# Sharing one low-rank partial product between the two token halves of a tile

## The chip, the cores and the metric

The kernel runs on one core of one Trainium2 chip. The metric is the device time of one execution in microseconds (us), as the median of several runs. A profile of one execution stands beside it: the span from the first to the last instruction of the core, what each engine did in it, and who waited for whom.

## The reference

The input is u, 2 x 1024 tokens of width 512. The network is

```
x = u
x = x + 0.5 * ffn(layernorm(x))
x = x + s4(layernorm(x))          # convolution of length 512 along the width, plus D * input
x = x + 0.5 * ffn(layernorm(x))   # the same weights again

def qlinear(x, q, scale, A, B):   # q: integers 0..15
    return x @ ((q - 7.5) * scale * 0.005).T + 0.02 * (x @ A @ B)
def ffn(x):                       # 512 -> 1376 -> 512, low rank R = 32
    h = silu(qlinear(x, gate)) * qlinear(x, up)
    return qlinear(h, down)
```

What matters here is x @ A for the gate and the up projection together. The two matrices A have 32 columns each. The kernel calls this product P.

## The kernel before, in words

The 2048 tokens are four tiles of 512. Each tile goes through the feed-forward part twice, so there are N2 = 8 tile passes, n = 0 to 7; the convolution is worked in between, in the passes 2 to 5. This text calls a pass simply a tile. A tile has four sub-tiles of 128 tokens, i = 0 to 3.

Every number that TensorE multiplies is split into a high and a low part in fp16. For A both parts lie side by side in `a_w`, 128 columns in all (gate high, up high, gate low, up low; 4 * R), one block of rows for each 128 of the width.

Tiles 0 and 1 are multiplied plainly (`plain_blocks`). From tile 2 on (`FAST = 2`) gate and up are computed by a scheme with seven products of half-size blocks (`fast_blocks`). Its operands lie transposed in `xT`: B11 and B21 are the upper and lower half of the width for the first 256 tokens, B22 is the lower half for the second 256 tokens, and T1 is the upper half for the second 256 tokens minus B11. So the second tokens' upper half isn't there itself; it is T1 + B11.

A tile n is two stages. In the first, 11 blocks m of 128 inner features are multiplied (L1402, `part`), with the low-rank terms added by `low_rank` (L1365) from `PT`, the transposed P of the tile. In the second, the down stage, `down_pass` (L1323) multiplies the hidden features, four sub-tiles j with a wide and a narrow half each. Between the passes of the down stage stand small pieces of work, in an order written out by hand for each engine in its function `tile`:

- `pd_high` (ACT, L616), `pd_split` (DVE, L904), `pd_transpose` (PE, L1335), `pd_copy` (ACT, L624), `down_low` (PE, L1342): the low-rank term of the down projection, for each j. `down_low` needs what `pd_copy` wrote.
- `p_product(n + 1, i)` (PE, L1288): P of the next tile, sub-tile i, into one bank of PSUM. `p_high` (ACT, L597) takes its high part into `p_stack`, `p_split` (DVE, L897) its low part, and SP's queue then transposes it by a DMA into `PT`. `p_product(i)` waits until `p_split(i - 1)` is done, since both use the same bank. In the tiles from 2 on the four sub-tiles are taken in the order 0, 2, 1, 3 of the tokens (`sub`), so i = 0 and 2 are of the first 256 tokens, i = 1 and 3 of the second.
- `down_read`, `down_add` (DVE, L943, L955, L958): the residual sum into X. `conv_product` and `conv_add`: the convolution. `conv_stats`, `ln_stats`: sums for the normalisations.

Each engine takes its instructions strictly in order. At the end of the down stage the order on ACT is p_high(3), pd_copy(3); after the second pass it is p_high(1), pd_copy(1). On PE, `down_low(3)` is the last instruction ahead of the next tile's first block.

Of the kernel before, what the change touches and what calls it, by code (L numbers as in the profile page):

```python
# [19 lines left out]
P = 128  # L20
# [12 lines left out]
def s4_macaron(nc, x_d, state_d, step_d, gq_d, uq_d, dq_d, scales_d, ds_d, a_d, b_d, da_d, db_d,  # L33
# [39 lines left out]
    with ExitStack() as ctx:  # L73
# [125 lines left out]
        tab = view(ring, 0, P, 2, KH, L)  # L199
        phase, ptmp, toep = view(ring, 4096, P, 2, KH, P), view(ring, 5120, P, 2, P), view(ring, 5376, P, L)  # L200

        cz16 = view(ring, 0, P, TS, 2, H, dt=F16)
        czs = view(ring, 2048, P, 2, H)
        czT = view(ring, 3072, P, TS, 2, KH, P, dt=F16) if False else \
# [51 lines left out]
        class Ffn:  # L256
# [3 lines left out]
            def __init__(self):  # L260
                def s(what):
                    return sem(f"ffn_{what}")

                def two(what):
                    return [s(f"{what}_{b}") for b in range(2)]

                self.agg, self.var, self.rstd = s("ln_aggregated"), s("ln_var"), s("ln_rstd")
                self.zs, self.zhi, self.z16 = s("zs"), s("z_hi"), s("z16")

                self.z_d, self.z_t = s("z_differences"), s("z_sums")  # L270
                self.zq_hi, self.zq_lo = s("z_quarters_hi"), s("z_quarters_lo")
                self.tp0, self.xT0 = s("first_x_transposed"), [s(f"first_xT{j}_ready") for j in range(4)]
                self.xT = [s(f"xT_sub{j}_ready") for j in range(4)]
                self.xTq = two("xT_quarters_ready")
                self.p_mm, self.p_hi, self.p_stack = s("p_mm"), s("p_hi"), s("p_stack")
                self.p_t0, self.PT0 = s("first_p_transposed"), s("first_PT_ready")
                self.PT = two("PT_ready")
                self.pd_mm, self.pd_hi, self.pd_stack = s("pd_mm"), s("pd_hi"), s("pd_stack")
                self.pd_t, self.pd_out = s("pd_transposed"), s("PdT_ready")

                self.g_mm, self.gl_mm, self.u_mm, self.ul_mm = s("g_mm"), s("gl_mm"), s("u_mm"), s("ul_mm")
                self.tg, self.tu = two("gate_scaled"), two("up_scaled")

                self.p1, self.p5, self.p6, self.p3, self.p7 = (s(f"product_{i}") for i in (1, 5, 6, 3, 7))
                self.t11, self.t5, self.t12, self.t21 = (s(f"sum_{i}_copied") for i in ("11", "5", "12", "21"))
                self.up_s, self.gate_s = s("up_sums_scaled"), s("gate_sums_scaled")
                self.lr_gate, self.lr_up = s("low_rank_gate_mm"), s("low_rank_up_mm")
# [291 lines left out]
        def _(act):  # L579
# [8 lines left out]

            def p_high(n, i):

                act.wait_ge(f.p_mm, n * TS + i + 1)
                if n * TS + i < TS + 2:
                    after(act, f.p_t0, n * TS + i - 1)
                else:
                    act.wait_ge(f.PT[i % 2], (n - 1) * 32 + i // 2 * 16)
                for slot, part in ((0, 0), (3, 0), (2, 1)):
                    last = nc.scalar.activation(  # L597
                        p_stack[:, i % 2, :, slot, :],
                        p_bank(n, i)[:, part * 2 * R:(part + 1) * 2 * R].rearrange("p (g r) -> p g r", g=2),
                        ACT.Copy, scale=P_SCALE / (Z_SCALE * A_SCALE))  # L600
                last.then_inc(f.p_hi, 1)

# [204 lines left out]
        def _(dve):  # L807
# [73 lines left out]
            def z_step(n, m):  # L881
# [9 lines left out]
                elif m in (4, 10):  # L891
                    z_sums(n, m // 10)

            def p_split(n, i):

                dve.wait_ge(f.p_hi, n * TS + i + 1)
                V.scalar_tensor_tensor(p_stack[:, i % 2, :, 1, :],  # L897
                                       p_bank(n, i)[:, 0:2 * R].rearrange("p (g r) -> p g r", g=2),
                                       P_SCALE / (Z_SCALE * A_SCALE), p_stack[:, i % 2, :, 0, :],
                                       ALU.mult, ALU.subtract).then_inc(f.p_stack, 1)  # L900

# [15 lines left out]
            def h_low(n, m):  # L917
                b, r = m % 2, rows[m]
                dve.wait_ge(f.hhi[b], uses(n, m) + 1)
                V.tensor_tensor(hT[0:r, m, 1, :], h32[0:r, b, :], hT[0:r, m, 0, :], ALU.subtract)\  # L920
                    .then_inc(f.hlo[b], 1)
# [99 lines left out]
            def tile(n):  # L1021

                more, s4, c = n + 1 < N2, n + 1 == FAST, conv_group(n)
                (plain_blocks if n < FAST else fast_blocks)(n)
                h_low(n, M - 1)
                pd_split(n, 0)
                down_read(n, 0)
                pd_split(n, 1)
                if more:
                    p_split(n + 1, 0)  # L1030
                down_read(n, 1)
                down_add(n, 0)
                if n == 0:
                    s4_b_copy()
                if more:
                    p_split(n + 1, 1)
                pd_split(n, 2)
# [12 lines left out]
                    s4_scale()  # L1050
                if c is not None:
                    conv_add(c * TS + 2)
                if more:
                    p_split(n + 1, 2)
                pd_split(n, 3)
# [3 lines left out]
                    s4_vectors()  # L1059
                if s4:  # L1060
                    s4_split()
                if more:
                    p_split(n + 1, 3)
                down_read(n, 3)
# [189 lines left out]
        def _(pe):  # L1254
# [14 lines left out]
            def p_product(n, i):  # L1269

                s = sub(n, i)
                if n == 0:
                    pe.wait_ge(f.xT0[i], 1)
                elif n < FAST:
                    pe.wait_ge(f.xT[i], n * 16)
                else:
                    pe.wait_ge(f.xTq[i // 2], (n - FAST + 1) * 32)
                if not (n == 0 and i < 3):
                    pe.wait_ge(f.p_stack, i - 2 if n == 0 else n * TS + i)
                if n < FAST:  # L1280
                    terms = [(xT_plain[:, a, c, s * P:(s + 1) * P], c) for c in range(KH) for a in range(2)]
                else:
                    j = s % 2
                    ops = ((B11, 0), (B21, 2)) if s < 2 else ((T1, 0), (B11, 0), (B22, 2))
                    terms = [(xT[:, a, 2 * op + k, j * P:(j + 1) * P], c + k)
                             for op, c in ops for k in range(2) for a in range(2)]
                for t, (x, c) in enumerate(terms):
                    last = mm(p_bank(n, i)[:, 0:4 * R], x, a_w[:, c, :], start=(t == 0), stop=(t == len(terms) - 1))  # L1288
                last.then_inc(f.p_mm, 1)

            def p_transpose(j):
# [355 lines left out]
```

## Time and profile before

| | |
|---|---|
| Median of 3 runs | 592.99 us (592.35 to 594.93) |
| The profiled execution's own time | 592.97 us |
| Span of the profiled execution | 591.2 us |
| Granted TensorE clock, mean | 0.994 |
| PE busy | 570.9 us, 97% |
| DVE busy | 410.8 us, 69% |
| ACT busy | 303.3 us, 51% |
| POOL busy | 238.5 us, 40% |

PE is TensorE's multiplications, PEld its weight loads, DVE VectorE, ACT ScalarE, POOL GpSimd, SP the engine that issues most DMAs. In the rows below, "L897 DVE ... p_stack<-banks,p_stack" is one instruction of line 897 that writes p_stack from PSUM (banks) and p_stack. An arrow in square brackets says how long the engine stood idle before the instruction and what ended that. Matmuls are pipelined, so the end of one is modelled and overlaps the next: the time that a matmul costs is read from the starts.

### The profile page before, as it was taken

The numbers are of one execution on the slowest core, as the hardware profiler recorded it, in microseconds if no ns is written. First come the engines' busy times: TensorE is split into PE (matmuls) and PEld (weight loads), VectorE is DVE, ScalarE is ACT, GpSimd is POOL, SyncE is SP. The second block draws the span as 40 slices with busy tenths as digits, with TensorE's granted clock in tenths as the row PEclk, the third lists the DMA queues.
The fourth block names the chain that finished last, engine by engine and source line by source line (L and its number), as shares of the span: only waits on it lengthen the run. The fifth ranks groups of instructions, "written<-read, shape, count | busy, mean of one in ns | idle before, by whom it ended". The sixth has DMA issues, their size and how long they took to land.

```text
span 591.2 us, 12188 instructions
## 1 busy us (share of the span) xinstructions
PE 570.9 (97%) x4674; PEld 439.0 (74%) x4674; DVE 410.8 (69%) x768; ACT 303.3 (51%) x748; POOL 238.5 (40%) x245
## 2 busy tenths in 40 slices
PE   7799999999989999999999999999999999999997
PEld 6444675436568887788878887788877888788975
DVE  6578876697288885698675995469844788446544
ACT  5576322655117871288514785057831586236621
POOL 5447802031204881058800597015850367105510
PEclk8999999999999999999999999999999999999999
DMA  8991302203300066000730019200190201630001
GB/s 274 373 372 23 72 10 58 95 0 67 65 14 1 1 82 125 11 1 7 129 72 10 2 19 147 42 11 1 19 183 11 77 1 32 104 136 17 1 2 72
DMA packets 86009, 40.50 MB, mean 69 GB/s; under 512 B 74592, under 2 KB 78880, under 8 KB 85952
## 3 DMA queue, kind: packets, MB, share of 16 engines
q1 hardware_dynamic: 85136, 39.59, 28.4%
q8 instruction: 37, 0.61, 0.4%
q10 hardware_dynamic: 816, 0.14, 0.1%
q14 instruction: 20, 0.16, 0.1%
HBM read 17.43 MB, written 4.19 MB: 37 GB/s over the span
## 4 chain that ended last, share of the span: by engine, by line
PE 88%; SPq 3%; DVE 3%; DMA 2%; ACT 2%; issue 1%; DVEq 1%; POOL 0%; ACTq 0%
PE banks L1402 34%; PE banks L1323 28%; PE banks L1383 9%; PE banks L1365 5%; PE banks L1536 4%; PE banks L1288 3%; DMA X<-in_x 2%; PE banks L1342 2%; SPq L333 1%; PE banks L1359 1%; PE banks L1519 1%; SPq L332 1%; ACT p_stack L597 1%; DVEq L817 1%; ACT PdT L624 0%
## 5 line engine op out<-in xcount | busy, mean ns | idle before, releaser
L1402 PE MATMUL banks<-xT,w 128*128 128x256 f16 (+1 forms) x1848 | 223.1, 273 | 1.3 <-DVE ring L955 1.3
L1402 PEld LDWEIGHTS banks<-xT,w 128*128 128x128 f16 (+1 forms) x1848 | 182.0, 100 | 22.7 <-issue 1.7
L1323 PE MATMUL banks<-dw,hT 128*128 128x256 f16 (+3 forms) x1408 | 184.4, 286 | 0.0
L1323 PEld LDWEIGHTS banks<-dw,hT 128*128 128x128 f16 (+1 forms) x1408 | 135.4, 98 | 34.5 <-issue 0.6
L914 DVE SCALAR_TENSOR_TENSOR work<-banks,work 128x512 f32<-128x512 f32 (+1 forms) x88 | 60.6, 689 | 53.4 <-PE banks L1365 24.9
L1383 PE MATMUL banks<-xT,w 128*128 128x512 f16 (+1 forms) x336 | 80.7, 385 | 2.1 <-ACT work L646 1.1
L446 POOL TENSOR_TENSOR rstd<-veps,minus_half 128x1 f32<-128x1 f32 x32 | 20.7, 648 | 151.5 <-DVE veps L820 151.3
L510 POOL TENSOR_SCALAR hT<-work 128x512 f16<-128x512 f32 x60 | 38.0, 633 | 89.0 <-DVE work L914 88.9
L513 POOL TENSOR_TENSOR hT<-work,hT 128x512 f16<-128x512 f32 x60 | 71.0, 1183 | 5.0
L1383 PEld LDWEIGHTS banks<-xT,w 128*128 128x128 f16 (+1 forms) x336 | 33.3, 101 | 43.2 <-ACT work L646 3.1
L597 ACT ACTIVATE p_stack<-banks 128x64 f16<-128x64 f32 x96 | 14.6, 225 | 88.0 <-PE banks L1288 84.6
L520 POOL TENSOR_TENSOR z<-zs,z 128x1024 f16<-128x1024 f32 (+1 forms) x24 | 46.9, 1964 | 25.5 <-ACT z L671 25.5
L928 DVE SCALAR_TENSOR_TENSOR banks<-banks,scales,work 128x512 f32<-128x512 f32 (+1 forms) x66 | 49.5, 750 | 2.2 <-PE banks L1402 2.2
L935 DVE SCALAR_TENSOR_TENSOR banks<-banks,scales,work 128x512 f32<-128x512 f32 (+1 forms) x66 | 49.5, 750 | 0.7 <-ACT work L728 0.4
L714 ACT ACTIVATE work<-banks,scales 128x256 f32<-128x256 f32 (+1 forms) x66 | 31.3, 475 | 26.6 <-PE banks L1402 26.6
L728 ACT ACTIVATE work<-banks,scales 128x256 f32<-128x256 f32 (+1 forms) x66 | 31.2, 473 | 25.2 <-PE banks L1402 25.0
L653 ACT ACTIVATE work<-banks 128x512 f32<-128x512 f32 (+1 forms) x66 | 39.4, 597 | 5.2 <-PE banks L1365 5.2
L635 ACT ACTIVATE banks<-banks,scales 128x512 f32<-128x512 f32 (+1 forms) x44 | 28.9, 657 | 22.7 <-PE banks L1383 22.5
L897 DVE SCALAR_TENSOR_TENSOR p_stack<-banks,p_stack 128x64 f16<-128x64 f32 x32 | 7.2, 224 | 47.9 <-ACT p_stack L597 47.9
L710 ACT ACTIVATE work<-banks,scales 128x256 f32<-128x256 f32 (+1 forms) x66 | 31.3, 474 | 7.1 <-PE banks L1402 7.1
L717 ACT ACTIVATE work<-banks,scales 128x256 f32<-128x256 f32 (+1 forms) x66 | 31.3, 474 | 0.0
L904 DVE SCALAR_TENSOR_TENSOR pd_stack<-banks,pd_stack 128x32 f16<-128x32 f32 x32 | 6.0, 189 | 36.2 <-ACT pd_stack L616 36.0
(167 smaller groups left out, 708.8 us busy)
## 6 DMA issues: line engine op xcount, KB each, us to landing
out_x<-X SPq DMA_DIRECT2D x16, 256.0 KB, 2.7
X<-in_x SPq DMA_DIRECT2D x1, 2048.0 KB, 14.0
ring<-in_tables SPq DMA_DIRECT2D x1, 2048.0 KB, 9.1
ring<-in_gate_q_t SPq DMA_DIRECT2D x2, 768.0 KB, 13.0
hT<-in_up_q_t SPq DMA_DIRECT2D x2, 768.0 KB, 13.0
work<-in_b SPq DMA_DIRECT2D x2, 688.0 KB, 9.5
X<-in_x SPq DMA_DIRECT2D x4, 256.0 KB, 5.5
X<-in_x SPq DMA_DIRECT2D x1, 1024.0 KB, 12.5
```

The source lines that it names most:

```text
L510: pool.tensor_scalar(hT[0:r, m, 0, :], h32[0:r, b, :], 1.0, 0.0, ALU.mult, ALU.add)\
L513: pool.tensor_tensor(hT[0:r, m, 1, :], h32[0:r, b, :], hT[0:r, m, 0, :], ALU.subtract)\
L520: pool.tensor_tensor(z16[:, j, 1, ops, :], zs[:, ops, :], z16[:, j, 0, ops, :], ALU.subtract)\
L653: nc.scalar.activation(silu[0:r, b, :].rearrange("p (c t) -> p c t", c=2), gate_sums(m), ACT.Silu, scale=LR_OUT).then_inc(f.silu[b], 1)
L710: nc.scalar.activation(t_up[s][0:r, 0, :], sums, ACT.Copy, scale=scales[0:r, 1, m:m + 1])\
L714: nc.scalar.activation(t_gate[s][0:r, 1, :], bank[4 * s + 1][0:r, 0:HH], ACT.Copy, scale=scales[0:r, 0, m:m + 1]).then_inc(f.t5, 1)
L914: V.scalar_tensor_tensor(shape(h32[0:r, b, :]), up, H_SCALE * LR_OUT, shape(silu[0:r, b, :]), ALU.mult, ALU.mult).then_inc(f.h[b], 1)
L928: V.scalar_tensor_tensor(up_sums(m), up_sums(m), scales[0:r, 1, m:m + 1], t_up[s][0:r, :, :], ALU.mult, ALU.add).then_inc(f.up_s, 1)
L935: V.scalar_tensor_tensor(gate_sums(m), gate_sums(m), scales[0:r, 0, m:m + 1], t_gate[s][0:r, :, :], ALU.mult, ALU.add).then_inc(f.gate_s, 1)
L1323: last = mm(acc(j)[:, 1 - c, 0:width], hT[0:rows[m], m, a, j * P:(j + 1) * P], dw[0:rows[m], m, src], start=(m == 0 and a == 0), stop=(m = ...
L1383: last = mm(dst[0:r, :], wg[:, c, cols], xT_plain[:, a, c, :], start=(c == 0 and a == 0), stop=(c == KH - 1 and a == 1))
L1402: last = mm(dst[0:r, 0:HH], w[:, blocks + k, cols], xT[:, a, 2 * op + k, :], start=(first and k == 0 and a == 0), stop=(k == 1 and a == 1) ...
```

## The change

For the tiles from 2 on, the upper half of A times B11 is multiplied once for each 128 first tokens and stays in PSUM, in the first 128 columns of the bank. The own part of each sub-tile goes beside it, in columns of its own: for i = 0 and 2 the lower half (B21), for i = 1 and 3 T1 and B22. The product of i = 1 uses the B11 sums that i = 0 left, that of i = 3 those that i = 2 left. An even i has 8 matmuls as before, an odd i has 8 for 12.

The sum of both parts is made by DVE in a new step, `p_sum(n + 1, i)`: it copies the own part from PSUM to `p32` in SBUF, waits for that copy, and adds the shared part from PSUM to it. `p_high` and `p_split` then read `p32`. `p_high` waits for `p_summed` where it waited for `p_mm`. `p_sum` stands on DVE directly ahead of each `p_split` of a tile from 2 on.

```diff
@@ view of SBUF @@
+        p32 = view(ring, 7168, P, 4 * R)
@@ p_high(n, i) @@
-                act.wait_ge(f.p_mm, n * TS + i + 1)
+                if n < FAST:
+                    act.wait_ge(f.p_mm, n * TS + i + 1)
+                else:
+                    act.wait_ge(f.p_sum, (n - FAST) * TS + i + 1)
+                src = p_bank(n, i) if n < FAST else p32
@@ new, on DVE @@
+            def p_sum(n, i):
+
+                k = (n - FAST) * TS + i
+                dve.wait_ge(f.p_mm, n * TS + i + 1)
+                after(dve, f.p_hi, n * TS + i)
+                own = slice(4 * R * (1 + i % 2), 4 * R * (2 + i % 2))
+                V.tensor_copy(p32, p_bank(n, i)[:, own]).then_inc(f.p_own, 1)
+                dve.wait_ge(f.p_own, k + 1)
+                V.tensor_tensor(p32, p_bank(n, i)[:, 0:4 * R], p32, ALU.add).then_inc(f.p_sum, 1)
@@ tile(n) on DVE, and likewise for 1, 2 and 3 @@
+                if fast:
+                    p_sum(n + 1, 0)
                 if more:
                     p_split(n + 1, 0)
@@ p_product(n, i) on PE @@
                 if n < FAST:
-                    terms = [(xT_plain[:, a, c, s * P:(s + 1) * P], c) for c in range(KH) for a in range(2)]
+                    last = sums(0, [(xT_plain[:, a, c, s * P:(s + 1) * P], c) for c in range(KH) for a in range(2)])
+                elif i % 2 == 0:
+                    sums(0, half(B11, 0))
+                    last = sums(1, half(B21, 2))
                 else:
-                    j = s % 2
-                    ops = ((B11, 0), (B21, 2)) if s < 2 else ((T1, 0), (B11, 0), (B22, 2))
...
+                    last = sums(2, half(T1, 0) + half(B22, 2))
                 last.then_inc(f.p_mm, 1)
```

The order of instructions on three engines shows what has moved. First PE at the end of the down stage of tile 3, before. L1288 is the product of sub-tile 3, L1335 and L1342 are `pd_transpose(3)` and `down_low(3)`, and L1402 is the first block of the next tile. What an instruction waits for stands in brackets.

```order
L1288 MATMUL banks_3<-a_w,xT 128x128 [waits ffn_p_stack,ffn_xT_quarters_ready_1]
L1288 MATMUL banks_3<-a_w,xT 128x128 x11
L1335 MATMUL banks_1<-ident,pd_stack 128x128 [waits ffn_dsum,ffn_PdT_ready,ffn_pd_stack]
L1323 MATMUL banks_5<-dw,hT 128x256 x4
L1342 MATMUL banks_1<-db_w,PdT 128x512 [waits ffn_dsum,ffn_PdT_ready]
L1402 MATMUL banks_3<-xT,w 128x256 [waits conv_out,ffn_p_stack,ffn_silu_0,ffn_xT_quarters_ready_1,ffn_xT_quarters_ready_0]
```

The rows after the change are the same but for the count: the first product of the group is followed by 7 and not 11.

```order
L1310 MATMUL banks_3<-a_w,xT 128x128 [waits ffn_p_stack,ffn_xT_quarters_ready_1]
L1310 MATMUL banks_3<-a_w,xT 128x128 x7
```

ACT at the same place, after the change: L624 is `pd_high(3)` there, L605 `p_high(3)` and L632 `pd_copy(3)`.

```order
L624 ACTIVATE pd_stack<-banks_5 128x32 [waits ffn_pd_transposed,ffn_pd_mm]
L624 ACTIVATE pd_stack<-banks_5 128x32 x2
L605 ACTIVATE p_stack<-ring 128x2x32 [waits ffn_PT_ready_1,ffn_p_summed]
L605 ACTIVATE p_stack<-ring 128x2x32 x2
L632 ACTIVATE PdT<-banks_1 128x128 [waits ffn_dl_mm,ffn_pd_transposed]
```

The order on ACT is as before; `p_high` waits for DVE's sum in place of PE's product, and `pd_copy` still stands behind it.

DVE in the second half of the down stage of tile 1, before. L897 is `p_split` of the sub-tiles 2 and 3, and L1210 to L1213 are `s4_split`, which is done once, in this tile.

```order
L897 SCALAR_TENSOR_TENSOR p_stack<-banks_1,p_stack 128x2x32 [waits ffn_p_hi]
L904 SCALAR_TENSOR_TENSOR pd_stack<-banks_5,pd_stack 128x32 [waits ffn_pd_hi]
L1210 RECIPROCAL k_scale<-k_scale 128x1 [waits s4_kernel_scale_ready]
L1211 TENSOR_SCALAR ring<-ring,k_scale 128x512 [waits dve_s4_step]
L1212 CAST ring<-ring 128x512 [waits dve_s4_step]
L1213 TENSOR_TENSOR ring<-ring 128x512 [waits dve_s4_step]
L897 SCALAR_TENSOR_TENSOR p_stack<-banks_1,p_stack 128x2x32 [waits ffn_p_hi]
L943 TENSOR_TENSOR work<-banks_5,d_scale 128x512 [waits ffn_dsum,ffn_d_mm_1]
L955 SCALAR_TENSOR_TENSOR ring<-banks_3,work 128x512 [waits ffn_d_read_1,ffn_x_updated,ffn_dl_mm]
```

And after the change, where L916 is `p_split`:

```order
L908 COPY ring<-banks_1 128x128 [waits ffn_p_hi,ffn_p_mm]
L910 TENSOR_TENSOR ring<-banks_1,ring 128x128 [waits ffn_p_own_copied]
L916 SCALAR_TENSOR_TENSOR p_stack<-ring,p_stack 128x2x32 [waits ffn_p_hi]
L923 SCALAR_TENSOR_TENSOR pd_stack<-banks_5,pd_stack 128x32 [waits ffn_pd_hi]
L1238 RECIPROCAL k_scale<-k_scale 128x1 [waits s4_kernel_scale_ready]
L1239 TENSOR_SCALAR ring<-ring,k_scale 128x512 [waits dve_s4_step]
L1240 CAST ring<-ring 128x512 [waits dve_s4_step]
L1241 TENSOR_TENSOR ring<-ring 128x512 [waits dve_s4_step]
L908 COPY ring<-banks_1 128x128 [waits ffn_p_hi,ffn_p_mm]
L910 TENSOR_TENSOR ring<-banks_1,ring 128x128 [waits ffn_p_own_copied]
L916 SCALAR_TENSOR_TENSOR p_stack<-ring,p_stack 128x2x32 [waits ffn_p_hi]
L962 TENSOR_TENSOR work<-banks_5,d_scale 128x512 [waits ffn_dsum,ffn_d_mm_1]
```

Two instructions stand ahead of each `p_split`, and ACT's `p_high(3)`, which waited for PE alone before, comes behind all of `s4_split` through them. Over the six tiles these are 48 matmuls fewer and 48 instructions on DVE more.

## Rows read from the trace of the kernel before

**Rows 1.** The page: PE's busy time, and the shares of the last chain by engine.

```profile
PE 570.9 (97%) x4674; PEld 439.0 (74%) x4674; DVE 410.8 (69%) x768; ACT 303.3 (51%) x748; POOL 238.5 (40%) x245
PE 88%; SPq 3%; DVE 3%; DMA 2%; ACT 2%; issue 1%; DVEq 1%; POOL 0%; ACTq 0%
```

**Rows 2.** Waits, whole span: who waited for whom, us in total, times, longest.

```profile
PEld banks L1342 <- ACT PdT L624: 10.1, 31, 0.5
```

**Rows 3.** Timeline, tile 3 around P's sub-tile 1: start, us, engine, line.

```profile
301.46 0.83 PE L1288 MATMUL banks<-a_w,xT 128*128 128x128 f16 x12
...
302.13 0.22 PE L1335 MATMUL banks<-ident,pd_stack 128*128 128x128 f16 x1
...
302.19 0.71 PE L1323 MATMUL banks<-dw,hT 128*128 128x320 f16 x4
302.33 0.46 ACT L597 ACTIVATE p_stack<-banks 128x64 f16<-128x64 f32 x3 [4.88 <-PE banks L1288]
302.66 0.30 ACT L624 ACTIVATE PdT<-banks 128x128 f16<-128x128 f16 x1
...
303.00 0.10 PEld L1342 LDWEIGHTS banks<-db_w,PdT 128*128 128x128 f16 x1 [0.45 <-ACT PdT L624]
303.01 0.39 PE L1342 MATMUL banks<-db_w,PdT 128*128 128x512 f16 x1
```

**Rows 4.** Timeline, tile 3 around P's sub-tile 3, end of the tile.

```profile
317.51 0.30 ACT L624 ACTIVATE PdT<-banks 128x128 f16<-128x128 f16 x1
...
317.85 0.10 PEld L1342 LDWEIGHTS banks<-db_w,PdT 128*128 128x128 f16 x1 [0.50 <-ACT PdT L624]
```

**Rows 5.** DVE's groups by line and form: count, busy us, mean ns, idle before.

```profile
L955 DVE SCALAR_TENSOR_TENSOR ring<-banks,work 128x512 f32<-128x512 f32 x32 | 22.0, 689 | 2.2
...
L897 DVE SCALAR_TENSOR_TENSOR p_stack<-banks,p_stack 128x64 f16<-128x64 f32 x32 | 7.2, 224 | 47.9 <-ACT p_stack L597 47.9
...
L1150 DVE COPY cs<-banks 128x32 f32<-128x32 f32 x1 | 0.2, 181 | 0.0
```

**Rows 6.** ACT's groups by line and form, a source in PSUM and in SBUF.

```profile
L653 ACT ACTIVATE work<-banks 128x512 f32<-128x512 f32 x60 | 35.8, 597 | 0.7 <-PE banks L1365 0.7
L640 ACT ACTIVATE hT<-work 128x512 f16<-128x512 f32 x20 | 12.6, 631 | 12.1 <-DVE work L914 12.1
```

**Rows 7.** Timeline, tile 6, which has no convolution: P's sub-tiles 1 to 3.

```profile
514.65 0.22 DVE L897 SCALAR_TENSOR_TENSOR p_stack<-banks,p_stack 128x64 f16<-128x64 f32 x1 [1.47 <-ACT p_stack L597]
...
521.98 0.23 DVE L897 SCALAR_TENSOR_TENSOR p_stack<-banks,p_stack 128x64 f16<-128x64 f32 x1 [2.00 <-ACT p_stack L597]
...
523.15 0.77 PEld L1288 LDWEIGHTS banks<-a_w,xT 128*128 128x128 f16 x12
```

**Rows 8.** Timeline, end of tile 1 with `s4_split`.

```profile
170.87 0.23 DVE L897 SCALAR_TENSOR_TENSOR p_stack<-banks,p_stack 128x64 f16<-128x64 f32 x1 [1.12 <-ACT p_stack L597]
...
172.15 0.83 PE L1288 MATMUL banks<-a_w,xT 128*128 128x128 f16 x12
172.42 0.69 DVE L1213 TENSOR_TENSOR ring<-ring 128x512 f16<-128x512 f32 x1
173.01 0.46 ACT L597 ACTIVATE p_stack<-banks 128x64 f16<-128x64 f32 x3 [1.91 <-PE banks L1288]
...
174.46 0.69 DVE L955 SCALAR_TENSOR_TENSOR ring<-banks,work 128x512 f32<-128x512 f32 x1
...
175.40 0.82 PE L1402 MATMUL banks<-xT,w 128*128 128x256 f16 x6 [1.32 <-DVE ring L955]
```

**Rows 9.** Stretches: length, busy us of PE, PEld, DVE, ACT, POOL (count), PEclk, DMA.

```profile
98.40:101.10 2.70, 1.87 (x17) 1.82 (x16) 2.23 (x5) 1.16 (x2) 1.56 (x2) 1.00 0.12 26
101.20:102.50 1.30, 1.30 (x7) 0.56 (x7) 0.00 (x0) 0.00 (x0) 0.04 (x1) 0.93 0.83 247
102.50:105.00 2.50, 2.50 (x7) 0.88 (x6) 0.00 (x0) 1.18 (x2) 0.00 (x0) 0.50 1.02 377
105.00:106.00 1.00, 1.00 (x4) 0.39 (x3) 0.00 (x0) 0.00 (x0) 0.00 (x0) 0.64 1.04 397
```

More of the change, by code:

```diff
@@ L274, in __init__ @@
                 self.xTq = two("xT_quarters_ready")
+                self.p_own, self.p_sum = s("p_own_copied"), s("p_summed")
                 self.p_mm, self.p_hi, self.p_stack = s("p_mm"), s("p_hi"), s("p_stack")
@@ L598, in p_high @@
                         p_stack[:, i % 2, :, slot, :],
-                        p_bank(n, i)[:, part * 2 * R:(part + 1) * 2 * R].rearrange("p (g r) -> p g r", g=2),
+                        src[:, part * 2 * R:(part + 1) * 2 * R].rearrange("p (g r) -> p g r", g=2),
                         ACT.Copy, scale=P_SCALE / (Z_SCALE * A_SCALE))
@@ L892, in z_step @@
                     z_sums(n, m // 10)
+            def p_sum(n, i):
[6 more added lines that the diff above has]
+                V.tensor_tensor(p32, p_bank(n, i)[:, 0:4 * R], p32, ALU.add).then_inc(f.p_sum, 1)
             def p_split(n, i):
                 dve.wait_ge(f.p_hi, n * TS + i + 1)
+                src = p_bank(n, i) if n < FAST else p32
                 V.scalar_tensor_tensor(p_stack[:, i % 2, :, 1, :],
-                                       p_bank(n, i)[:, 0:2 * R].rearrange("p (g r) -> p g r", g=2),
+                                       src[:, 0:2 * R].rearrange("p (g r) -> p g r", g=2),
                                        P_SCALE / (Z_SCALE * A_SCALE), p_stack[:, i % 2, :, 0, :],
@@ L1025, in tile @@
                 h_low(n, M - 1)
+                fast = more and n + 1 >= FAST
                 pd_split(n, 0)
@@ L1034, in tile @@
                     s4_b_copy()
+                if fast:
+                    p_sum(n + 1, 1)
                 if more:
@@ L1052, in tile @@
                     conv_add(c * TS + 2)
+                if fast:
+                    p_sum(n + 1, 2)
                 if more:
@@ L1061, in tile @@
                     s4_split()
+                if fast:
+                    p_sum(n + 1, 3)
                 if more:
@@ L1279, in p_product, with sums, half @@
                     pe.wait_ge(f.p_stack, i - 2 if n == 0 else n * TS + i)
+                def sums(out, terms):
+                    for t, (x, c) in enumerate(terms):
+                        last = mm(p_bank(n, i)[:, out * 4 * R:(out + 1) * 4 * R], x, a_w[:, c, :], start=(t == 0),
+                                  stop=(t == len(terms) - 1))
+                    return last
+                def half(op, c):
+                    return [(xT[:, a, 2 * op + k, s % 2 * P:(s % 2 + 1) * P], c + k) for k in range(2) for a in range(2)]
                 if n < FAST:
-                    terms = [(xT_plain[:, a, c, s * P:(s + 1) * P], c) for c in range(KH) for a in range(2)]
-                else:
-                    j = s % 2
-                    ops = ((B11, 0), (B21, 2)) if s < 2 else ((T1, 0), (B11, 0), (B22, 2))
[L1285 to L1288, printed above, removed]
+                    last = sums(0, [(xT_plain[:, a, c, s * P:(s + 1) * P], c) for c in range(KH) for a in range(2)])
+                elif i % 2 == 0:
+                    sums(0, half(B11, 0))
+                    last = sums(1, half(B21, 2))
+                else:
+                    last = sums(2, half(T1, 0) + half(B22, 2))
                 last.then_inc(f.p_mm, 1)
```

## The prediction, made before the changed kernel was run

> **What bounds the kernel now.** I read the page first: PE is busy 97% of the span and makes up 88% of the chain that ended last [rows 1]. So each matmul taken away counts in full, if nothing comes in its place. Then I asked where PE does stand still, because an edit that takes 4 matmuls from a group can be lost in one short stall. The view of the waits shows it at once: the largest wait of PE's weight loads on another engine is that of `down_low` (L1342) for ACT's `pd_copy` (L624), 31 times, 0.5 us at most [rows 2]. That is a wait in the very stretches where the change works.
>
> The timeline of tile 3 shows why it is long there. P's product for sub-tile 1 issues from 301.46; PE goes on to `pd_transpose` and four matmuls of the down pass, the last steps it can take. ACT waits for the product, runs `p_high` from 302.33, and only then, in its order, `pd_copy` at 302.66, which ends at 302.96; the weights of `down_low` load at 303.00, after 0.45 us of idle weight loader [rows 3]. `pd_copy` itself had its input at 302.35, when the transpose had ended (302.13 + 0.22): it is late because it stands behind `p_high`. At sub-tile 3 the same chain ends at 317.81 and lets `down_low` go at 317.85, after 0.50 us [rows 4]; then comes the next tile. So in each fast tile two chains, product - `p_high` - `pd_copy` - `down_low`, are on the path already, with nothing to spare.
>
> **What the change removes.** 12 matmuls of 128 columns take 302.13 - 301.46 = 0.67 us from start to start, 56 ns each [rows 3]. It takes away 4 at i = 1 and 4 at i = 3, 0.22 us a site; 48 in six tiles would be 2.7 us if PE alone counted.
>
> **What it adds.** Two DVE instructions, 128 columns wide, stand between the product and `p_high`. No row has this width. A line through L897 (64 wide, 224 ns) and L955 (512 wide, 689 ns) has 1.04 ns a column, so the add is 290 ns; from the copy of 32 columns (181 ns) the same slope gives 281 ns [rows 5]. Each handover costs some 35 ns: the transpose-to-load case is `pd_copy`'s end at 302.96 to the load at 303.00, and PE's product to ACT is alike, so the one to DVE takes the place of the old one and two are new (copy to add, add to ACT). The pair is 0.28 + 0.29 + 0.07 = 0.64 us. The bounds: two copies of 32 columns would be 0.36 + 0.07 = 0.43 us, two instructions of 512 columns 1.38 + 0.07 = 1.45 us. I take 0.64, since 128 lies much nearer to 64 than to 512. `p_high` now reads SBUF: ACT's 512-wide instruction takes 631 ns from there for 597 from PSUM [rows 6], so 0.03 us more.
>
> The Trainium skill, page "VectorE: DVE Perf Modes", section "The TRN2 errata — SBUF-src ops pay a fixed extra latency per instruction", prices a VectorE instruction from PSUM at 120 cycles plus one for each element and ScalarE's at 224 from SBUF for 172 from PSUM. As an estimate by that page copy and add would be 0.52 us and not 0.57, `p_high` 0.04 us later, and my sum below 0.5 us smaller. Its figure for 64 columns would be 192 ns where the trace has 224 [rows 5], so I stay with the rows.
>
> **The sites.** At i = 1 of tile 3, `p_high` starts 0.64 - 0.22 later and `pd_copy` ends 0.45 us later (0.64 + 0.03 - 0.22); `down_low` goes with it, and with `down_low` everything behind it on PE. The same at i = 3. DVE is free when the product arrives: it stood idle before all of its 32 `p_split`s together 47.9 us [rows 5], in tile 6 at i = 1, the tightest, 1.47 us before 514.65 [rows 7], of which `p_high` and the handovers take some 0.5 and the pair of i = 0 before it pushes it 0.63, so about 0.1 is left after the 0.22 saved. The pairs at i = 0 and i = 2 are hidden: behind i = 0 nothing of PE is due for four microseconds of down pass, and behind i = 2 stands `p_product(3)`, which waits for `p_split(2)`. That ends at 522.21, with the pair at 522.88, and the product's first load is at 523.15 [rows 7]: 0.27 us are left. Behind the waiting `p_sum` on DVE stand `p_split`, `pd_split` or `down_read`, and `down_add`; DVE stood there before too, waiting for ACT, so they come later by the pair and no more, and PE's next need of each is later than that. SP's transposes of P move with `p_split`, and `PT` is first read in the next tile's second block.
>
> So each of the tiles 2 to 6 costs 2 x 0.45 = 0.90 us, and five of them 4.5 us.
>
> **Tile 1** is dearer. Its i = 1 costs 0.45 as above. At i = 2 `p_split` (170.87) comes 0.67 later again, and with it `s4_split`, which stands behind it on DVE and ended at 173.11 (172.42 + 0.69), just about when `p_high(3)` started, 173.01 [rows 8]. Before, `p_high(3)` did not depend on it. Now `p_sum(3)` comes behind it: `s4_split` ends at 173.11 + 0.44 + 0.64 = 174.19, the pair starts some 0.08 before (DVE instructions overlap by that) and `p_high(3)` starts at 174.11 + 0.64 = 174.75, 1.74 us later. The 4 matmuls saved at i = 3 gain nothing there, as PE's product (172.15) is done long before. `pd_copy`, `down_low` and `down_add` (174.46) follow, and PE's first block waits for that sum before and after (175.40, 1.32 us idle) [rows 8]. Tile 1 costs 1.77 us with ACT's 0.03.
>
> **The sum:** 13 pairs on the path (two in each of five tiles, three in tile 1) at 0.67 = 8.7 us, less 11 savings of 0.22 = 2.4 us: +6.3 us. The profiled execution took 592.97 us, 0.02 under the median of the runs, so no correction is due: 599.2 us, 1.05% slower.
>
> **The rivals.**
> - *PE alone counts.* The chains are hidden, only the 48 matmuls go: 592.97 - 2.7 = 590.3 us. For it speaks PE's 97%. Against it: the pair would have to be under 0.22 us, which is where a site turns, and two copies of even 32 columns are 0.36 us [rows 5]. Place: `down_low` at i = 1 and 3. Chance 5%.
> - *Half is given back.* The delay at i = 3 is made up in the next tile, because PE waits there for something that did not move. Then five sites go: 6.3 - 5 x 0.45 = +4.0, 597.0 us. Against it: `down_low` is the last step before the tile, and PE's stalls inside the fast blocks are tiny beside 570.9 us busy. Chance 12%.
> - *The clock falls at the end of tile 1.* PE is to stand there almost idle from about 173.6 to 177.1 but for one `down_low`. After 98.40 to 101.10, a stretch in which PE had only tiny matmuls and gaps, the granted clock was 0.93, then 0.50 (the level of 1.2 GHz), then 0.64 over the next 4.8 us [rows 9]; that lost 1.3 x 0.07 + 2.5 x 0.50 + 1.0 x 0.36 = 1.7 us. The sum becomes +8.0: 600.9 us. The Trainium skill, "TensorE: Matmul & The Clock Gate", section "Part 1: The HAM clock gate (the 'warmup' mystery)", has the throttled state as the default that activity lifts; by that rule 600.9 is the answer if the gap is long enough, and the trace shows such a fall once. Chance 15%.
> - *The pair is longer*, 0.8 us or more, by the wait for its own copy or a slower copy from PSUM: 13 x 0.16 = 2.1 more, 601.3 us, and at 0.9 `p_product(3)` of tile 6 begins to wait too. Chance 8%.
>
> **How the numbers follow.** The forecast has 60%: 599.2 us, its own range 597.9 to 600.5 with the pair 0.1 us either way (13 x 0.1). The range to hold the time 8 times in 10 goes from 596.9, which takes in half given back, to 601.2, which takes in the fall of the clock. A measurement of this kernel can tell 0.5%, 3 us, from no change: slower means above 595.96 and faster below 590.03. Forecast, clock, longer pair and two thirds of the second rival are slower: 91%. 7% are within, with most of the first rival, which lies at -0.45%. Faster 2%.
>
> **What would show it.** The wait of `down_low`'s load on `pd_copy` rises from 10.1 us by 0.67 x 11 plus 1.5 in tile 1, to about 19 us. From the first matmul of the odd P products to `down_low` there are 1.55 us in tile 3 now (301.46 to 303.01) and about 2.0 after. Copy and add show 0.28 and 0.29 us. PE's idle time before the first block of tile 2 stays at 1.3 us, with another 1.9 us before `down_low`. The fast blocks themselves, from the second block on, last as long as before. I would be wrong if `down_low` no longer waits for `pd_copy` (then less), if copy and add together take under 0.45 us, or if the granted clock behind tile 1 falls under 1.00.

## The result and the profile after

The changed kernel takes 602.19 us (median of 4 runs, 601.35 to 602.88) for 593.72 us of the kernel before on the same chip: a ratio of 1.0154, 95% interval 1.0133 to 1.0176. It is slower, as forecast, but by more: the forecast counted 6.3 us on top of 592.97, and 602.19 is 9.2 us above that number (8.5 us above the median of this comparison). 602.2 lies above the range, which ended at 601.2. The traced execution took 602.22 us, its span is 600.5 us. Of all executions below, one of e8 and one of e12 took 850 us at a mean granted clock of 0.65; the ratios leave them out.

First the waits of PE's weight loads on other engines, changed kernel, whole span: the row that answers to [rows 2]. L1377 is `down_low` and L632 `pd_copy`.

```profile
PEld banks L1377 <- ACT PdT L632: 19.9, 31, 2.2
```

It was 10.1 us with at most 0.5 in one place; 19 were forecast. The only other wait that grew by as much as a microsecond is at L1293, ahead of the fast tiles, in code that the change leaves as it was (PE's wait there is 5.4 us for 4.3). So the loss is in this one wait, and in what the wait brings about. Here is the timeline of the changed kernel in tile 3 around P's sub-tile 1, the stretch of [rows 3].

```profile
306.50 0.61 PE L1310 MATMUL banks<-a_w,xT 128*128 128x128 f16 x8
...
306.94 0.22 PE L1370 MATMUL banks<-ident,pd_stack 128*128 128x128 f16 x1
...
307.14 0.29 DVE L908 COPY ring<-banks 128x128 f32<-128x128 f32 x1 [0.48 <-PE banks L1310]
307.47 0.29 DVE L910 TENSOR_TENSOR ring<-banks,ring 128x128 f32<-128x128 f32 x1
307.80 0.55 ACT L605 ACTIVATE p_stack<-ring 128x64 f16<-128x64 f32 x3 [4.54 <-DVE ring L910]
308.25 0.26 ACT L632 ACTIVATE PdT<-banks 128x128 f16<-128x128 f16 x1
308.38 0.23 DVE L916 SCALAR_TENSOR_TENSOR p_stack<-ring,p_stack 128x64 f16<-128x64 f32 x1 [0.61 <-ACT p_stack L605]
...
308.56 0.10 PEld L1377 LDWEIGHTS banks<-db_w,PdT 128*128 128x128 f16 x1 [1.18 <-ACT PdT L632]
```

Eight matmuls in place of twelve, then copy and add at 0.29 us each, then `p_high` and `pd_copy`, and only then the load, after 1.18 us idle for 0.45 before. From the start of the copy to that of `p_high` pass 0.66 us. From the start of `p_high` to that of `pd_copy` pass 0.45 us, where they were 0.33 (302.33 to 302.66, [rows 3]), and `pd_copy` itself takes 0.26 for 0.30. So a site costs 0.66 + 0.12 - 0.04 = 0.74 us and saves 0.22.

The chain that ended last gives the start of each tile's first block: start, us, line, count. The kernel before:

```profile
175.40 5.18 PE banks L1402 x46
246.89 5.04 PE banks L1402 x46
318.25 5.04 PE banks L1402 x46
389.61 5.04 PE banks L1402 x46
460.95 5.04 PE banks L1402 x46
525.19 5.08 PE banks L1402 x46
```

And the changed kernel:

```profile
176.72 7.90 PE banks L1437 x46
251.95 5.04 PE banks L1437 x46
324.31 5.04 PE banks L1437 x46
396.69 5.04 PE banks L1437 x46
469.06 5.04 PE banks L1437 x46
534.38 5.09 PE banks L1437 x46
```

Each of these rows is one tile, from 2 to 7. A tile of the steady part takes 72.37 us (from 324.31 to 396.69, and from there to 469.06) for 71.35 before: 1.02 more, with 0.90 forecast. Tile 2 is another matter: 75.23 us for 71.49, 3.74 more, of which 2.72 are in the first 46 matmuls alone, 7.90 us for 5.18. The stretches of the changed kernel around them say why (length, busy us of PE, PEld, DVE, ACT, POOL with counts, granted TensorE clock, DMA):

```profile
173.10:176.60 3.50, 0.39 (x1) 0.10 (x1) 2.68 (x7) 0.71 (x4) 0.00 (x0) 0.84 0.13 26
176.60:182.20 5.60, 5.48 (x26) 3.94 (x27) 1.70 (x5) 1.42 (x3) 0.55 (x1) 0.50 0.02 6
182.20:184.60 2.40, 2.40 (x24) 2.14 (x22) 1.95 (x3) 1.51 (x4) 0.00 (x0) 0.98 0.00 0
```

PE had one matmul in 3.5 us, and the granted clock was 0.50, the level of 1.2 GHz, for the whole of the next 5.6 us; half of PE's 5.48 busy us there is 2.7 us. That was a rival with 15%. Only the traced execution shows where the clock fell; its mean over the span is 0.987, those of the other three are 0.990, 0.993 and 0.991. The end of tile 1 in the changed kernel, which answers to [rows 8]:

```profile
172.99 0.69 DVE L1241 TENSOR_TENSOR ring<-ring 128x512 f16<-128x512 f32 x1
173.59 0.28 DVE L908 COPY ring<-banks 128x128 f32<-128x128 f32 x1
173.91 0.29 DVE L910 TENSOR_TENSOR ring<-banks,ring 128x128 f32<-128x128 f32 x1
174.24 0.55 ACT L605 ACTIVATE p_stack<-ring 128x64 f16<-128x64 f32 x3 [2.57 <-DVE ring L910]
...
175.00 0.39 PE L1377 MATMUL banks<-db_w,PdT 128*128 128x512 f16 x1 [1.92 <-ACT PdT L632]
175.78 0.69 DVE L974 SCALAR_TENSOR_TENSOR ring<-banks,work 128x512 f32<-128x512 f32 x1
...
176.72 5.49 PE L1437 MATMUL banks<-xT,w 128*128 128x256 f16 x25 [1.33 <-DVE ring L974]
```

The copy comes directly behind `s4_split`, as forecast, and PE stands still 1.92 and 1.33 us with one matmul between.

### The profile page after: what moved, and what is told of

It is laid out like the page before. It is cut to its first block, busy times and chain, and to the rows that moved or that the text cites. A ratio compares the mean times of both kernels' runs of the same rounds, so it can differ in the third digit from the quotient of the medians.

```text
span 600.5 us, 12164 instructions
## 1 busy us (share of the span) xinstructions
PE 570.0 (95%) x4626; PEld 436.7 (73%) x4626; DVE 424.0 (71%) x816; ACT 305.1 (51%) x748; POOL 238.6 (40%) x245
## 4 chain that ended last, share of the span: by engine, by line
PE 88%; DVE 6%; ACT 2%; issue 2%; DMA 1%; DVEq 1%; POOL 0%; SPq 0%; ACTq 0%
PE banks L1437 34%; PE banks L1358 27%; PE banks L1418 10%; PE banks L1400 5%; PE banks L1571 4%; PE banks L1310 2%; PE banks L1377 2%; PE banks L1394 1%; ACT p_stack L605 1%; PE banks L1554 1%; DMA X<-in_x 1%; DVE ring L910 1%; DVE ring L908 1%; DVEq L825 1%; DVE stats L824 0%
## 5 line engine op out<-in xcount | busy, mean ns | idle before, releaser
L1437 PE MATMUL banks<-xT,w 128*128 128x256 f16 (+1 forms) x1848 | 225.8, 275 | 1.3 <-DVE ring L974 1.3
L605 ACT ACTIVATE p_stack<-ring 128x64 f16<-128x64 f32 x72 | 13.1, 245 | 80.0 <-DVE ring L910 80.0
L624 ACT ACTIVATE pd_stack<-banks 128x32 f16<-128x32 f32 x96 | 11.8, 196 | 37.1 <-PE banks L1358 37.1
```

Of the source, the lines that this page charges most:

```text
L1437: last = mm(dst[0:r, 0:HH], w[:, blocks + k, cols], xT[:, a, 2 * op + k, :], start=(first and k == 0 and a == 0), stop=(k == 1 and a == 1) ...
```

## The experiments

The theory: the pair of DVE instructions lies on the chain product, `p_high`, `pd_copy`, `down_low` at i = 1 and 3, and PE waits for its end; behind tile 1 the stretch gets so empty that the clock falls. The rivals: DVE's load as such, and a slow first block from some other source. All ratios are to the kernel before on the same chip. The times of the tiles and of the clock are from one traced execution of each kernel.

**e1: the pair without the saving.**

```diff
-                own = slice(4 * R * (1 + i % 2), 4 * R * (2 + i % 2))
+                own = slice(0, 4 * R)
...
-                V.tensor_tensor(p32, p_bank(n, i)[:, 0:4 * R], p32, ALU.add).then_inc(f.p_sum, 1)
+                V.tensor_tensor(p32, p_bank(n, i)[:, 0:4 * R], p32, ALU.max).then_inc(f.p_sum, 1)
...
                 elif i % 2 == 0:
-                    sums(0, half(B11, 0))
-                    last = sums(1, half(B21, 2))
+                    last = sums(0, half(B11, 0) + half(B21, 2))
                 else:
-                    last = sums(2, half(T1, 0) + half(B22, 2))
+                    last = sums(0, half(T1, 0) + half(B11, 0) + half(B22, 2))
```

> The changed kernel with all 40 matmuls back: each product is multiplied whole, as before the change, and the two DVE instructions stay (the second takes the maximum of the sum and its own copy, so the values are those of before). Theory (the pair lies on the chain product, p_high, pd_copy, down_low, and the removed matmuls shorten the same chain): each of 11 sites is 0.22 us later than in the changed kernel, 602.2 + 2.4 = 604.6 us, and P's first matmul to down_low in tile 3 takes 2.3 us. Rival (the removed matmuls were hidden behind waits and brought nothing): 602.2 us.

Measured 604.07 us, ratio 1.0189 (1.0151 to 1.0227). The edit puts back 48 matmuls (4674 on the page for 4626), not the 40 of the expectation. In the chain of its trace:

```profile
176.76 5.18 PE banks L1436 x46
...
322.53 5.04 PE banks L1436 x46
395.36 5.04 PE banks L1436 x46
468.20 5.04 PE banks L1436 x46
```

A steady tile takes 72.83 us, 0.46 more than in the changed kernel: the eight matmuls are worth 56 ns each also behind the new wait, because they lie ahead of it on the chain. In the traced execution the clock did not fall behind tile 1, and the first 46 matmuls took 5.18 us, though PE stood idle 1.69 and 1.33 us there. So an execution can have nearly the same empty stretch without the fall. This one took 601.78 us at a mean clock of 0.996, the other three 603.57 to 605.50 us at 0.991. As an estimate from these means, 0.005 of 600 us is 3 us, about the difference; where the clock fell in those three is not shown.

**e2: the saving without the pair.**

```diff
-    ops = ((B11, 0), (B21, 2)) if s < 2 else ((T1, 0), (B11, 0), (B22, 2))
+    ops = ((B11, 0), (B21, 2)) if s < 2 else ((T1, 0), (B22, 2))
```

> The kernel before with B11 times A's upper half left out of the products of i = 1 and 3, so P of the second 256 tokens of the fast tiles is wrong in that part; nothing is added on DVE. Theory (48 matmuls at 56 ns each, all on PE's chain): 593.7 - 2.7 = 591.0 us. Rival (the chain over ACT starts from something else than PE's product, so they are worth nothing): 593.7 us.

This kernel leaves the upper half of A times B11 out of P for the second 256 tokens. Measured 590.53 us, ratio 0.9951 (0.9934 to 0.9967). A steady tile takes 70.90 us (317.89 to 388.79 in the chain), 0.45 less than 71.35. All that the removed matmuls give is 2.4 us of 593 by the medians, and with e1 the pairs cost 72.83 - 71.35 = 1.48 us a tile, 0.74 a site.

**e3: PE kept busy behind tile 1.**

```diff
                 pd_transpose(n, 3)
                 down_pass(n, 3, 1, LATE)
+                if s4:
+                    pe.wait_ge(s_tcopy, 1)
+                    for _ in range(28):
+                        mm(bank[0][:, P:2 * P], ident16[:, :], ident16[:, :], start=True, stop=True)
                 down_low(n, 3)
+                if s4:
+                    for _ in range(16): ...   # the same matmul
```

> The changed kernel with 28 dummy matmuls of 128 columns ahead of down_low(3) in tile 1 and 16 behind it, where PE stands idle for 1.9 and 1.3 us; they write to a bank that nobody reads. Theory (the granted clock fell behind tile 1 because PE stood there, and that cost 2.7 us): the clock stays at 1.00 in the first blocks of tile 2, 602.2 - 2.7 = 599.5 us. Rival (the slow first blocks come from elsewhere, data or DMA): 602.2 us, or more by what the dummies cost.

Measured 598.59 us, ratio 1.0093 (1.0062 to 1.0124), 3.6 us less than the changed kernel. The stretches that answer to those above:

```profile
173.10:176.80 3.70, 3.00 (x47) 2.53 (x44) 2.85 (x8) 0.71 (x4) 0.00 (x0) 1.00 0.19 37
176.80:182.20 5.40, 5.31 (x49) 4.80 (x50) 3.73 (x8) 3.04 (x7) 0.55 (x1) 1.00 0.01 2
```

In the chain of its trace stands tile 2's row:

```profile
176.89 5.18 PE banks L1437 x46
```

The tile starts as late as before the edit (176.89), its first 46 matmuls take 5.18 us, and 44 matmuls of no use make the kernel faster: all four executions (598.39 to 599.81 us) lie below all four of the changed kernel. With PE busy the fall is gone, and with it 2.7 us in the traced execution. As e1's trace had no fall without any filling, one trace alone would not show this; two of e3's executions have a mean clock of 1.000, so they have no fall anywhere, and none of the changed kernel's is above 0.993. The traced executions differ by 2.4 us. The medians differ by more, 3.6 us, because e3's traced execution was its slowest: it still has two falls ahead of tile 1 (0.50 from 10 to 12 us and from 102 to 104 us) that the two at 1.000 cannot have.

**e4: `s4_split` behind `down_add(3)` on DVE.**

```diff
-                if s4:
-                    s4_split()
                 if fast:
                     p_sum(n + 1, 3)
...
                 down_add(n, 3)
+                if s4:
+                    s4_split()
```

> The changed kernel with s4_split moved behind down_add(3) on DVE in tile 1, so that p_sum(3) no longer stands behind it. Theory: p_sum(3) starts 0.9 us earlier and PE's idle stretch is that much shorter. If the clock then holds, 602.2 - 0.9 - 2.7 = 598.6 us; if it falls all the same, 601.3 us. Rival (tile 1 is not limited by DVE's order but by PE and ACT): 602.2 us.

Measured 601.08 us, ratio 1.0130 (1.0096 to 1.0165). From P's last product to `down_low` 2.06 us for 3.02 (174.18 to 176.24, and 171.98 to 175.00): the 0.96 us were those of DVE's order. The clock fell in the traced execution all the same, at a smaller price, 6.85 us for the first 46 matmuls. So the order on DVE cost what was expected, and of the two cases named for the clock it was the worse one.

**e5: a single add at i = 1 and 3.**

```diff
+                if i % 2 == 0:
+                    V.tensor_copy(pb11, p_bank(n, i)[:, 0:4 * R]).then_inc(f.p_own, 1)
+                dve.wait_ge(f.p_own, k // 2 + 1)
+                V.tensor_tensor(p32, p_bank(n, i)[:, own], pb11, ALU.add).then_inc(f.p_sum, 1)
```

> The changed kernel, but the shared B11 part is copied to SBUF once, by the p_sum of i = 0 and 2; the p_sum of i = 1 and 3 is then a single add of its own part from PSUM to that copy. Theory (every nanosecond between the product and p_high of i = 1 and 3 is PE's): copy and handover, 0.29 + 0.03 = 0.32 us, go at 12 sites, 3.9 us less; 602.2 - 3.9 = 598.3 us, and up to 2.7 us less again if the clock then holds behind tile 1. From P's first matmul to down_low in tile 3 0.32 us less. Rival (DVE's instructions cost as load, whichever site they stand at): half of the 24 copies go, some 1.5 us less, 600.7 us.

Measured 598.83 us, ratio 1.0080 (1.0049 to 1.0111). A steady tile takes 71.72 us (321.94 to 393.66), 0.65 less than in the changed kernel and twice the 0.32 us of copy and handover. The first 46 matmuls of tile 2 take 6.85 us, so the clock did not hold behind tile 1.

**e6: the sum back into PSUM.**

```diff
-    V.tensor_tensor(p32, p_bank(n, i)[:, 0:4 * R], p32, ALU.add)
+    V.tensor_tensor(p_bank(n, i)[:, own], p_bank(n, i)[:, 0:4 * R], p32, ALU.add)
```

> The changed kernel, but the add writes its sum back to the own columns of the PSUM bank, so p_high and p_split read PSUM as before the change. Theory (p_high's three instructions take 0.55 us from SBUF and took 0.46 from PSUM, and the site grew by that too): 13 times 0.09 to 0.12 us less, 602.2 - 1.4 = 600.8 us, and p_high back at 0.46 us. Rival (the longer p_high is overlapped with pd_copy behind it): 602.2 us.

Measured 601.28 us, ratio 1.0131 (1.0103 to 1.0159); the medians are 0.9 us apart and the intervals overlap, so the trace has to decide. Its group of `p_high`, all from PSUM, and below it that of the changed kernel, from SBUF (count, busy us, mean ns, idle before):

```profile
L605 ACT ACTIVATE p_stack<-banks 128x64 f16<-128x64 f32 x96 | 14.6, 225 | 94.2 <-DVE banks L910 80.9 <-PE banks L1310 9.9 <-PE banks L1331 3.4
```

```profile
L605 ACT ACTIVATE p_stack<-ring 128x64 f16<-128x64 f32 x72 | 13.1, 245 | 80.0 <-DVE ring L910 80.0
```

The three instructions in a row take 0.46 us again for 0.55, and a steady tile takes 72.21 us (323.00 to 395.21), 0.16 less. That is 0.08 a site, just the 0.12 less 0.04 that was read above from the starts of `p_high` and `pd_copy` and from `pd_copy`'s own time; `pd_copy` takes 0.30 us again.

**e7: the kernel before, with `pd_copy` ahead of `p_high`.**

```diff
-                if more:
-                    p_high(n + 1, 3)
                 pd_copy(n, 3)
+                if more:
+                    p_high(n + 1, 3)
...
-                        pe.wait_ge(f.p_stack, (n + 1) * TS)
...
+                    if m == 0:
+                        pe.wait_ge(f.p_stack, (n + 1) * TS)
                     part(m, gate_1, GATE2, T4, True)
```

> The kernel before with pd_copy(1) and pd_copy(3) ahead of p_high(1) and p_high(3) on ACT, and PE's wait for p_stack moved from a tile's first product to its second, the first that writes P's bank. Theory (down_low waits at these two sites because pd_copy stands behind p_high): the load's idle time falls from 0.45 and 0.50 to the 0.21 us that it is at j = 0 and 2, some 0.5 us a tile over 7 tiles, 593.0 - 3.6 = 589.4 us. Rival (down_low is late because of the transpose and the copy themselves): 593.0 us.

Measured 591.84 us, ratio 0.9967 (0.9955 to 0.9980). The wait that was 10.1 us, and the steady tiles of the chain:

```profile
PEld banks L1342 <- ACT PdT L624: 6.0, 31, 0.2
```

```profile
174.89 6.85 PE banks L1402 x46
...
318.28 5.09 PE banks L1402 x46
389.10 5.09 PE banks L1402 x46
459.92 5.09 PE banks L1402 x46
```

A tile takes 70.82 us for 71.35, as expected. The whole missed by 2.4 us. The 3.6 us expected took in a tile that gains nothing, as PE waits for dsum, DVE's sum into X, before tile 2 in any case; and the first blocks of tile 2 now ran at the low clock (6.85 us), so 1.7 us of the traced execution went that way. This fall came behind a single idle stretch of 1.83 us, in a kernel without the pair.

**e8: the changed kernel with the same edits**, PE's moved wait being for `p_summed`.

> The changed kernel with the same two edits; PE's wait at the second product is for p_summed, since nobody reads P's bank after the add. Theory: the pair is off PE's chain, the 0.22 us a site stay saved: 589.4 - 2.7 = 586.7 us, less what DVE's later down_add(3) costs at the start of the next tile (it may hold up the first product into bank 0 by 0.3 us a tile, 588.5 us). Rival (DVE's load or SP's later transposes of P cost the time, not the order on ACT): not under 598 us.

Measured 595.37 us, ratio 1.0033 (1.0009 to 1.0057). A steady tile takes 70.89 us (319.11 to 390.00 between first blocks), not 72.37: the pair is off PE's chain. But it is not 70.37 either. The timeline of the start of tile 4 shows the new wait:

```profile
319.73 0.22 DVE L916 SCALAR_TENSOR_TENSOR p_stack<-ring,p_stack 128x64 f16<-128x64 f32 x1 [0.61 <-ACT p_stack L605]
...
319.87 0.68 DVE L962 TENSOR_TENSOR work<-banks,d_scale 128x512 f32<-128x512 f32 x1
...
320.69 0.69 DVE L974 SCALAR_TENSOR_TENSOR ring<-banks,work 128x512 f32<-128x512 f32 x1
...
321.43 3.17 PEld L1437 LDWEIGHTS banks<-xT,w 128*128 128x128 f16 x30 [0.70 <-DVE ring L974]
```

`down_read(3)` and `down_add(3)` stand behind `p_split(3)` on DVE, which waits for `p_high`; the product into bank 0 waits for the sum. And the first 46 matmuls of tile 2 take 7.90 us, behind an idle stretch of 3.31 us. The expectation, 586.7 to 588.5 us, was missed by 7 to 9 us. The traced execution took 593.23 us, 6.5 above 586.7: 2.6 us are five tiles at 0.52 more than 70.37, 2.7 us are the clock, and 1.5 us are tile 1, which takes 27.01 us from P's first product to the next tile for 25.50 in e7. The median lies another 2.1 us above the traced execution, which is not explained. The rival, not under 598 us, is ruled out.

**e9: all of it, with sharing.** e8 with e5's single add and e4's order, and

```diff
+                down_read(n, 3)
                 if more:
                     p_split(n + 1, 3)
-                down_read(n, 3)
                 down_add(n, 3)
...
-                            pe.wait_ge(f.dsum, n * TS)    # tile 2, before its first product
...
+                        if n == FAST:
+                            pe.wait_ge(f.dsum, n * TS)    # before its second product
```

> All that helped, together with the shared product: pd_copy ahead of p_high on ACT at i = 1 and 3, PE's waits moved to the second product of a tile (in tile 2 also the one for dsum), the B11 part copied once, s4_split behind down_add(3), and on DVE down_read(3) ahead of p_split(3), so that down_add(3) is not late for the next tile. Theory (the sharing pays 0.45 us a tile once nothing stands on PE's chain): a tile takes 70.3 us, 0.5 less than in the kernel before with the swapped order (70.8), and with tile 1's shorter stretch 586 to 588 us. Rival (a new wait, as dsum's in e8, eats it): 70.9 us a tile and 590 us or more.

Measured 587.49 us, ratio 0.9908 (0.9888 to 0.9928): faster than the changed kernel by 14.7 us and than the kernel before by 0.9%. In its chain

```profile
313.51 5.02 PE banks L1438 x46
383.81 5.02 PE banks L1438 x46
454.10 5.09 PE banks L1438 x46
```

a tile takes 70.30 us, as expected, and the clock is 1.00 from 168 to 186 us. PE's idle time before the product that waits for dsum is 0.94 us here.

**e10: the same order without sharing.** These are the moves of e9 made in the kernel before.

> The same order of the engines without the shared product: the kernel before with pd_copy ahead of p_high, the moved waits, s4_split and down_read moved. Theory: a tile takes 70.7 us (0.45 more than with sharing, for 8 matmuls at 56 ns), the whole some 2.7 us more than the shared kernel of this pair, 589 to 590 us. Rival (sharing costs what it saves even off the path): the same time as the shared kernel.

Measured 591.23 us, ratio 0.9964 (0.9949 to 0.9980), 1.2 us above the 589 to 590 expected. Tiles take 71.08 us where 70.7 were expected. The waits of its weight loads name the cause, which is this order itself: the unshared `p_split(3)` reads P's bank, and behind `down_read` it comes too late for PE.

```profile
PEld banks L1402 <- DVE p_stack L897: 3.4, 6, 1.2
```

**e11: two more copies on DVE at each even i.**

```diff
+                if i % 2 == 0:
+                    V.tensor_copy(spare[0], p_bank(n, i)[:, own])
+                    V.tensor_copy(spare[1], p_bank(n, i)[:, own])
```

> The changed kernel with two more copies of 128 columns at each p_sum of i = 0 and 2, into SBUF that nobody reads, some 0.4 to 0.6 us of DVE at a site. Theory (the pairs at i = 0 and 2 are hidden behind passes of PE in the tiles 2 to 5): those tiles stay at 72.4 us; tile 1 is 0.4 to 0.6 us longer, since s4_split stands behind its i = 2, and tile 6, where only 0.1 to 0.3 us are left, a few tenths; 602.2 + 1 = 603.2 us. Rival (DVE's load as such costs time): each of the five tiles is about 0.8 us longer, 606 us or more.

Measured 602.36 us, ratio 1.0152 (1.0133 to 1.0170). The tiles 3 to 5 take 72.38 us (323.37, 395.75, 468.13), the changed kernel's 72.37, and tile 6 takes 65.73 (468.13 to 533.86) for 65.32. DVE's load as such costs nothing in the tiles 3 to 5. Where it was expected to show, it does: in tile 6, where the slack was narrow, 0.4 us, and in tile 1 another 0.4 us (27.65 us from P's first product to the next tile, for 27.26). The first 46 matmuls of tile 2 take 7.58 us.

**e12: e10 with `p_split(3)` ahead of `down_read(3)` again.**

> The kernel without sharing and in the same order as e10, but with p_split(3) ahead of down_read(3) on DVE again. Theory (in e10 PE waited for p_split(3) behind down_read(3), 3.4 us in all over 6 tiles): a tile goes back from 71.08 to 70.8 us, 591.2 - 1.5 = 589.7 us, still some 2 us above the shared kernel e9 (587.5). Rival (e9 is ahead of e10 by that order alone, not by the sharing): 587.5 us.

Measured 591.26 us, ratio 0.9976 (0.9960 to 0.9992). The trace has the tiles at 70.81 us, as expected, but the median did not go down. The early part of the kernel and its clock differ from execution to execution by more than the 1.4 us looked for, so this one is open. The granted clock points at where it went: the mean over the executions is 0.993 here and was 0.996 in e10, and 0.003 of 590 us is 1.8 us, an estimate; the two also ran on different chips. Against the shared kernel, e9, both plain orders are clearly slower: the intervals 0.9888 to 0.9928 and 0.9960 to 0.9992 don't touch. By the traces a tile is 0.51 us shorter with sharing (70.30 for 70.81). Five such tiles are 2.6 us of the 4.0 that the ratios are apart; the rest is not traced to a cause.

## Why the prediction was right in its way and short in its size

The step that failed is the clock, which the sum put at nothing; the other steps hold but for one size. The sum with measured sizes is: 13 pairs at 0.74 are 9.6 us, less 11 x 0.22 = 2.4, and 2.7 for the clock, and less 0.66 because tile 1's down stage began earlier in this execution (its first P product at 149.46 for 150.13 us): 9.2 us. The spans differ by 9.3 and the two profiled executions by 9.25. The 0.66 us are luck: the same product comes between 147.67 and 151.66 us in the traces, in code that is much the same, and without them the miss would have been larger. With the clock's 2.7 us alone the forecast would have been 601.9, with the dearer pair alone 600.1.

- *The sites are on the path* at i = 1 and 3, right: e1 and e2 separate pair and saving (0.74 and 0.22 us a site), e5 takes half the pair away and gets half a pair back, e7 and e8 take the order away and the site is gone.
- *The pairs at i = 0 and 2 are hidden*, right in the tiles 2 to 5 (e11). Tile 6 was called the tightest, with 0.1 to 0.27 us left; it takes 1.08 us more than before, the others 1.00 to 1.03, so even there hardly anything shows.
- *Copy and add, 281 and 290 ns*, right: 289 and 291.
- *ACT reads SBUF for 0.03 us more*, too small: that was the difference for one instruction, and `p_high` is three (x3 in [rows 3]). Three times 0.034 are 0.10 us, and the start of what follows moves by 0.12. `pd_copy`, which takes 0.26 us for 0.30, gives 0.04 back, so 0.08 are left for 0.03. With 0.02 us more in the handovers it makes 0.07 us a pair, 0.9 us in all.
- *Tile 1 is dearer by `s4_split`*, right: e4 gives 0.96 us back. Its cost is 1.32 + 0.66 = 1.98 us for 1.77, three times that same 0.07.
- *The clock falls*: this is the step that failed. I had worked out that PE would stand idle but for one matmul from 173.6 to 177.1 us, and had a row in which half clock followed a stretch of small matmuls and gaps, with PE far from idle (1.87 us busy of 2.70, [rows 9]). I gave it 15% all the same and left it out of the sum, and a granted clock under 1.00 behind tile 1 was named as a sign of being wrong. Of the six traces with the pair in tile 1 and the changed kernel's order on ACT and PE, without filling, five have the fall (the changed kernel, e4, e5, e6, e11) and one has not (e1). Of the five traces in which no pair stands there (the kernel before, e2, e7, e10, e12) only e7's has it.
- *The price of the fall*, 1.7 us, was too small as well: I took the loss of one earlier fall, where here the clock was at 0.50 for 5.6 us. It was not the only one either: in the same trace the granted clock is 0.54 from 10 to 12 us and 0.61 from 12 to 14 us, near the start of the kernel, which by the same reckoning loses 1.7 us too. In the other traces the first 46 matmuls lose 1.67 us (e4, e5, e6, e7), 2.40 (e11) or 2.72 (e8), so 1.7 to 2.7 us with a good chance would have been the honest term.

What decides whether the clock falls stays open. The length of PE's idle time alone does not: it fell behind 1.83 us in e7 and stayed behind 1.69 and 1.33 us in e1, and in the kernel before behind 0.22 and 1.32 us.

The Trainium skill, page "TensorE: Matmul & The Clock Gate", section "Part 1: The HAM clock gate (the 'warmup' mystery)", says that the throttled clock is the default and that activity lifts it. The changed kernel's trace agrees with it, 0.50 behind the empty stretch, and so does e3's, 1.00 behind the same stretch filled with dummies; e1's, 1.00 behind an almost equally empty stretch, shows that the empty stretch did not bring the fall each time.

## What to carry to other kernels

Ask first what PE waits for near an edit. Here eight matmuls of 56 ns in a tile were bought with four pairs of short instructions on DVE, and the two pairs for whose end PE was waiting counted in full, while the other two, but for one in tile 1 with `s4_split` behind it, cost next to nothing, whatever DVE's mean load was. A change of order that puts the awaited instruction ahead on its queue gave 0.53 us a tile (e7), a little more than the 0.45 us that the sharing saves, and after it, with the other waits moved too, the sharing paid (e9). Where a cost is read from one instruction, count how many stand in a row. When a change lengthens PE's idle time in one place, read what the granted clock did behind the emptiest stretches of the same trace, and put that into the sum.

## What the runs showed of the hardware that was not expected

- The extra that ACT pays for a source in SBUF came once for each instruction, and did not shrink with its width: 34 ns at 512 columns (631 for 597), and 0.09 us for three of 64 columns in a row (0.55 us for 0.46, 0.03 each).
- 44 matmuls of no use, 2.5 us of work in PE's gaps, made the traced execution 2.4 us faster (599.81 for 602.22) and the median 3.6 us (598.59 for 602.19), as the clock stayed at 1.00 behind tile 1.
- Nearly the same stretch was followed by half clock in one trace (the changed kernel) and by full clock in another (e1), and in e7 1.83 us without a matmul were followed by half clock (0.50 from 176 to 178 us; the first 46 matmuls took 6.85 us for 5.18).
